# Token attention: the maximum of wide heads is subtracted by the exponential itself, one head at a time, instead of by GpSimd

## The reference, cut to what matters

```python
scores = sips_alpha[0] * jnp.tanh(raw / sips_beta[0])
...
scores = scores + lam * hamming[:, None, :, :]
scores = scores + lat
causal = jnp.tril(jnp.ones((t, t), bool))
scores = jnp.where(causal[None, None], scores, -jnp.inf)
attn = jax.nn.softmax(scores, axis=-1)
out = jnp.einsum('bhij,bhjd->bhid', attn, v)
```

## Time and profile before

| | |
|---|---|
| runs, median (lowest to highest) | 4447.3 us (4442.75 to 4448.69) |
| profiled execution, its own time | 4451.65 us |
| span of its trace | 4449.6 us |
| mean granted TensorE clock | 0.966 |
| busy over the whole span | PE 89%, PEld 69%, DVE 69%, ACT 60%, POOL 41% |
| token attention in the trace | from about 50 to about 935 us |

### The profile page before, as it was taken

One profiled execution on the slowest core, in us unless ns is written; L12 is line 12 of the kernel. 1 busy time (PEld: TensorE's weight loads), 2 busy tenths in 40 slices (PEclk: granted clock), 3 DMA queues, 4 the chain that ended last, 5 costly groups with the idle time before them and its releaser, 6 DMA issues. The chain is left out here.

```text
span 4449.6 us, 104983 instructions
## 1 busy us (share of the span) xinstructions
PE 3951.2 (89%) x35227; PEld 3054.4 (69%) x35481; DVE 3057.0 (69%) x7210; ACT 2683.5 (60%) x6345; POOL 1837.7 (41%) x1769
## 2 busy tenths in 40 slices
PE   5999999938999988899999788999999999989999
PEld 4777777726666665566666546777767776669998
DVE  5888888867888865688888574555555555546666
ACT  4888888827777762477777325555555555533333
POOL 3555555446655541356565233333333333321111
PEclk9999999969999999999999899999999999999999
DMA  1000000010000001000000010000000000000000
GB/s 52 1 0 0 0 0 0 0 33 15 12 14 12 14 12 29 15 15 12 14 12 14 20 37 4 1 0 0 0 0 0 0 0 0 0 21 10 8 9 10
DMA packets 65662, 44.39 MB, mean 10 GB/s; under 512 B 39656, under 2 KB 54000, under 8 KB 65408
## 3 DMA queue, kind: packets, MB, share of 16 engines
q1 hardware_dynamic: 65568, 43.16, 3.9%
HBM read 13.53 MB, written 4.19 MB: 4 GB/s over the span
## 5 line engine op out<-in xcount | busy, mean ns | idle before, releaser
L1603 ACT ACTIVATE l_probs<-l_act,l_neg_max 128x128 f32<-128x128 f32 (+1 forms) x1024 | 415.9, 425 | 341.0 <-DVE l_neg_max L1560 338.7
L1544 POOL TENSOR_TENSOR l_probs<-l_probs,l_sums 128x512 f32<-128x512 f32 x384 | 391.5, 1041 | 452.6 <-DVE l_sums L1568 452.6
L1560 DVE TENSOR_REDUCE l_neg_max<-l_act 128x2 f32<-128x512 f32 (+1 forms) x384 | 247.0, 685 | 472.2 <-remote 193.7
L381 POOL TENSOR_TENSOR t_probs<-t_probs,t_neg_max 128x512 f32<-128x512 f32 x384 | 392.8, 1044 | 392.2 <-DVE t_neg_max L436 392.2
L429 DVE SCALAR_TENSOR_TENSOR t_probs<-t_tanh_qk,scalars_sb,t_dve 128x512 f32<-128x512 f32 x384 | 269.6, 743 | 88.3 <-ACT t_tanh_qk L532 38.2
L1920 ACT ACTIVATE e_hT<-e_act 128x512 f32<-128x512 f32 x256 | 153.0, 598 | 285.9 <-PE e_act L1939 285.9
L854 POOL TENSOR_TENSOR w_swappedQ<-w_rawQ,w_table 128x512 f32<-128x512 f32 x128 | 162.5, 1288 | 372.2 <-ACT w_rawQ L1032 361.1
L532 ACT ACTIVATE t_tanh_qk<-t_act,t_inv_beta 128x512 f32<-128x512 f32 x384 | 243.1, 684 | 91.7 <-PE t_act L597 91.3
L854 POOL TENSOR_TENSOR w_swappedK<-w_rawK,w_table 128x512 f32<-128x512 f32 x128 | 228.8, 1809 | 129.3 <-ACT w_rawK L1032 129.3
L1951 PEld LDWEIGHTS e_dve<-e_sb,e_hT 128*128 128x128 f32 x2048 | 269.4, 192 | 13.3
L1666 PE MATMUL l_dve<-ident_sb,l_probs 128*128 128x128 f32 x1536 | 211.3, 278 | 68.5 <-POOL l_probs L1544 67.6
(11 more groups left out here) (262 smaller groups left out, 10669.3 us busy)
## 6 DMA issues: line engine op xcount, KB each, us to landing
w_v_mid<-w_v SPq DMA_DIRECT2D x128, 130.0 KB, 2.3
m_h<-z SPq DMA_DIRECT2D x32, 128.0 KB
out<-x_sb SPq DMA_DIRECT2D x32, 128.0 KB, 1.8
m_h<-z SPq DMA_DIRECT2D x32, 127.0 KB
wqkv_sb<-L_ffn_wqkv SPq DMA_DIRECT2D x2, 768.0 KB, 6.0
m_h<-z SPq DMA_DIRECT2D x64, 0.2 KB
kv_up_sb<-L_attn_w_kv_up SPq DMA_DIRECT2D x1, 1024.0 KB, 4.9
e_sb<-L_ffn_w SPq DMA_DIRECT2D x1, 1024.0 KB, 5.4
```

What stands on the lines that cost most here:

```text
L381: nc.gpsimd.tensor_tensor(p, p, neg_max[:, j, 0:len(gs)].unsqueeze(2) .broadcast_to((P, len(gs), P * (t + 1))), ALU.add).then_inc(shifted. ...
L1544: nc.gpsimd.tensor_tensor(p, p, sums[:, at, 0:len(hs)].unsqueeze(2) .broadcast_to((P, len(hs), P * (t + 1))), ALU.mult).then_inc(divided.s ...
L1560: nc.vector.tensor_reduce(neg_max[:, units.index(name), 0:len(hs)], to_act.bank("s" + name, back)[:, :].rearrange("p (h j) -> p h j", h=le ...
L1603: ins = nc.scalar.activation(probs[:, at % SLOTS, s * width:(s + 1) * width], bank[:, s * width:(s + 1) * width], ACT.Exp, bias=neg_max[:, ...
```

## The change

For the wide units POOL does nothing any more: `shifted` counts the `i0` units alone. ACT waits for `maxed` in place of `shifted` and issues two exponentials of 128x256 for such a unit, each with one column of `neg_max` as its bias (a value per partition), in place of one of 128x512. The `i0` units stay as they were. The place of the exponentials in ACT's order is the same.

```diff
@@ -336,7 +336,8 @@
         maxed = Count(sem("maxed"), units, [], units)
-        shifted = Count(sem("shifted"), units, [], units)
+        by_pool = [name for name in units if unit(name)[2] == 0]
+        shifted = Count(sem("shifted"), by_pool, [], by_pool)
         exped = Count(sem("exped"), in_turns(EXP), [], units[:2 * (turns - EXP)], late(EXP))
@@ -372,7 +373,7 @@
-                        for name in twins(i) if back else []:
+                        for name in twins(i) if back and twins(i)[0] in by_pool else []:
@@ -519,6 +520,20 @@
+                def exponentials(name, seq):
+
+                    j = units.index(name)
+                    if name in by_pool:
+                        act.wait_ge(shifted.sem, shifted.done(name, seq))
+                        p = probs[:, j % SLOTS, :]
+                        nc.scalar.activation(p, p, ACT.Exp).then_inc(exped.sem, 1)
+                    else:
+                        act.wait_ge(maxed.sem, maxed.done(name, seq))
+                        for s in range(2):
+                            p = probs[:, j % SLOTS, s * T:(s + 1) * T]
+                            ins = nc.scalar.activation(p, p, ACT.Exp, bias=neg_max[:, j, s:s + 1])
+                        ins.then_inc(exped.sem, 1)
+
@@ -545,9 +560,7 @@
                         for name in twins(j) if seq else []:
-                            act.wait_ge(shifted.sem, shifted.done(name, seq))
-                            p = probs[:, units.index(name) % SLOTS, :]
-                            nc.scalar.activation(p, p, ACT.Exp).then_inc(exped.sem, 1)
+                            exponentials(name, seq)
```

## The result

| | before | after |
|---|---|---|
| median of 7 runs each | 4445.87 us (4442.75 to 4448.69) | 4458.21 us (4454.24 to 4466.01) |
| ratio, 95% interval | | 1.0031 (1.0019 to 1.0042) |
| profiled execution, its own time | 4451.65 us | 4457.7 us |
| its span | 4449.6 us | 4455.7 us |

The change makes the kernel slower by 12.3 us by the medians, 0.3%; the interval of the ratio does not reach 1. The forecast was slower by 18 us.

A forecast was written before the change was run, and what follows sets the result against it. The prediction took a ring of DVE, PE and ACT, through ACT's exponentials once, in turn 2, as the bound. 0.56 to 0.68, say 0.6 us per sequence over 31 sequences, gave 4447.3 + 18 = 4465 us, range 4449 to 4488.

The forecast's parts named there:

- POOL and its additions are off the path: Token attention: removing 8 of 12 POOL additions per sequence, 8.4 us of POOL, is worth nothing.
- Price of a half, 0.40 us: On ACT: each exponential of 256 columns with a bias per partition takes 0.40 us, 0.80 for a unit.
- What it replaces, 1.05 us for a pair: On ACT: two exponentials of 512 columns take 1.05 us, so a turn's two units cost 0.56 us more.
- Turn 4: ACT's added exponential time is hidden, because ACT afterwards waits for PE twice.
- turn 5 into 0: Turn 0's tanh comes later, but DVE has other work; hidden, with about 0.33 us left.
- turn 1 into 2: Turn 2's tanh is 0.3 to 0.5 us late; hidden by DVE's 0.80 and ACT's 0.68 us of idle.
- turn 2 into 3: ACT runs back to back up to turn 3's tanh, for which DVE waits; no cover, cost 0.56 us.
- Turn 1, 0 to 0.12 us: Turn 1's tanh is 0.15 to 0.28 us late, partly covered by DVE's slack; cost 0 to 0.12 us.
- ACT's idle time from 5.0 to 3.4 us: Profile after: ACT's idle time per sequence falls from 5.0 to about 3.4 us.
- rival 3: Clock dips fall on other turns as sequences lengthen, bringing 22 us back: faster, 4443 us; chance 0.05.
- DVE at the end of turn 5: DVE's two scalings, one held beside POOL's additions, stay at 1.34 us because turn 5's additions stay.
- rival 2: DVE's scaling at turn 5's end is freed from POOL's additions, at most 0.33 us usable: 4455 us; chance 0.03.

The follow-up runs named there:

- e3: Changed kernel, but the halves' bias is a column of zeros and POOL makes all its additions as before; 4461.42 us, ratio 1.0033 to the kernel before.
- e4: Changed kernel, but wide units' maxima are not subtracted and ACT makes one exponential of 512 columns; 4447.37 us, ratio 1.0002 to the kernel before.
- e9: Changed kernel with the exponentials of ACT's turn 2 in four pieces of 128 columns per unit; 4502.72 us, ratio 1.0129 to the kernel before.
- e1: Changed kernel with the bias only for the exponentials of ACT's turn 2, POOL adding for all other units; 4454.89 us, ratio 1.0024 to the kernel before.
- e2: Changed kernel with the bias for wide units except those of ACT's turn 2, which POOL keeps; 4447.9 us, ratio 1.0005 to the kernel before.
- e5: Changed kernel with the exponentials of turns 2 and 5 right after the tanh, before the value product's copy; 4447.94 us, ratio 1.0000 to the kernel before.
- e6: Changed kernel with no maximum subtracted for any unit and one exponential of 512 columns each; 4438.97 us, ratio 0.9986 to the kernel before.
- e11: Changed kernel, exponentials early in turns 2 and 5, DVE's copy before maxima in turns 3 and 4, its scalings before turn 5's maxima; 4416.08 us.
- e12: Kernel before with DVE's copy ahead of the maxima in turns 3 and 4 and its scalings ahead of turn 5's maxima; 4420.17 us, ratio 0.9937.

## Why the prediction was right, point by point

- *POOL and its additions are off the path; their removal is worth nothing.* Shown by e3 and e4.
- *Price of a half, 0.40 us.* Measured 0.400 from start to start. Of its parts the width is borne out by e9, 0.105 us for 128 columns where half of 217 ns was taken; the operand by itself was in no run.
- *What it replaces, 1.05 us for a pair.* Here the term was a little mis-sized: it was read in turn 1, ahead of a copy, while in turn 2 a tanh follows, and there the pair takes 1.09. So the turn costs 0.51 and not 0.56.
- *Turn 4, turn 5 into 0, and turn 1 into 2 are hidden; turn 2 into 3 has no cover.* Shown by e1 and e2 in both directions, and by e9 for more of the cost. Only one sentence goes too far: that turn 3's tanh did not wait for PE. Its scores were ready at the same moment (e5), so the exponentials were on the path for every microsecond added and for none taken away; the change adds, and the forecast did not hang on the difference. PE's transposes in turn 0 do wait for the exponentials now, 0.24 us in the sequence at 546.80, and PE's next wait covers it (0.76 us for DVE, at 549.12):

```profile
546.80 0.42 PEld L630 LDWEIGHTS t_dve<-ident_sb,t_probs 128*128 128x128 f32 x4 [0.24 <-ACT t_probs L534]
```

- *Turn 1, 0 to 0.12 us.* Nothing: e2 has 26.83. Together with the term above the sum of 0.6 us is 0.51 in the shorter kind of sequence and 0.42 in the longer (27.30 to 27.72). Why the longer kind takes 0.09 less was not tried; 0.07 of it lies between the tanhs of turns 0 and 1, 4.28 us in undisturbed sequences of before and 4.21 in e1 and in e5.
- *ACT's idle time from 5.0 to 3.4 us, an undisturbed sequence of 27.4.* (663.71 - 581.04) / 24 = 3.44 us, and 27.33.
- *The clock.* The prediction took the whole difference between 28.19 and 26.82 for one dip. That was wrong: 0.48 of it is the difference between the two kinds of sequence, 26.82 and 27.30, which is there at a granted clock of 1.00, and the dip's own cost is the rest, 0.8 to 0.9. But the mechanism of rival 3 was at work. The mean of the two kinds rose by 0.47 us, 14.4 us in 31 sequences. Dips at 0.82 us (28.12 to 27.30) fell from 8 to 3, and those left cost 28.87 - 27.33 = 1.54: 6.6 us before, 4.6 after. The two marks lie 10.9 us further apart (841.6 for 830.7), against 14.4 - 2.0 = 12.4 by this account. The 1.5 us left over were not traced further; the first and the last sequences, where the pipeline fills and drains, differ from the others in both traces. Outside the marks the traced execution of the changed kernel was 4.8 us shorter than that of before, so that the two spans differ by 6.1 us only; the medians are the ones to compare.
- *DVE at the end of turn 5.* The trace's row was read rightly and the additions of turn 5 did stay, so rival 2 was rightly unlikely. Its price was wrong: DVE's own work there is on the path, and e6 shows 0.26 and 0.74 us, 0.50 on average, where the prediction allowed at most 0.33.

The time came out 12.3 us over before, a little above the 9 us that the prediction took as what tells it from no change. Of the forecast's 18 us, 14.4 are the path; the terms of the pair and of turn 1 were too high by the rest, and the dips account for 2 us less again. That 12.4 us by this account and 12.3 by the medians agree to 0.1 is luck, since 1.5 us between the marks are open.

## What to carry to other kernels

An engine's idle time is not a budget: the same 0.5 us cost all of itself behind the copy that ACT had waited for, and nothing a few instructions earlier, where ACT stood waiting anyway. And a place without slack is not yet one where time can be won: two engines can be ready at the same moment, as ACT and PE were for turn 3. For each place where work is added, look for the next wait on the same engine, and at who waits for the instruction behind it. Last, ask of an operation that is on the path what it is held by, as DVE's scaling was by POOL's additions: moving it by one step was worth more than the change could have been.

## What the runs showed of the hardware

- An activation of 128x256 from SBUF with a bias per partition took 515 ns, and the next could start 0.400 us after it; of 128x128, 392 ns and 0.295 (2.36 us for eight). Two of 128x512 without an operand took 1.05 to 1.09 us. 128 columns more cost 0.105 us, so that by estimate (0.295 - 0.105) a fixed 0.19 us goes with each such instruction.
- A DVE scaling of 128x128 in SBUF takes 0.34 us alone and up to 1.10 us when it overlaps one of POOL's additions of 1.04 us; it then ends 0.08 us after the addition does. The Trainium skill (GPSIMD Engine Reference, 8. Key points) names a contention of the two engines for DVE instructions in a 2-port mode or with two SBUF inputs. No run here shows which mode the scaling was in. Here one instruction per sequence is held, and DVE's reductions of 512 columns, 668 to 684 ns in every kernel, show nothing of it. In e11 and e12 it was the other way round: beside DVE's addition of two SBUF inputs, 0.41 us, POOL's addition took 1.34 us in place of 1.04.
- The granted clock dipped to 1.2 GHz for 3.4 us between 3 and 16 times in this one stage, depending on the kernel, at 0.8 to 1.5 us each. PE's busy share does not sort them: e9 has the most dips with PE busy 26.35 us of the 28.46 ahead of one (93%), and the kernel before has 8 with 25.37 of 26.82 (95%), the changed one 3 with 25.77 of 27.32 (94%). What sets their number stays open. A change of 10 us in a kernel like this is of the size of what they do.
